# A graph network with attention on one core: own event lists for the first four and the last two iterations, the last batch's heads by transposes, its closing norm on VectorE

## The chip, the core and the metric

The kernel runs on one core of a Trainium2 chip. The metric is device microseconds of one execution. Engines are named as in the profile: PE (TensorE matmuls), PEld (its weight loads), DVE (VectorE), ACT (ScalarE), POOL (GpSimd) and SP, whose queue issues all the DMAs here.

## What is computed

Sixteen batches of 512 nodes with 128 features go through two layers, each with a residual and a layer norm.

```
def euler_step(h, _):                       # eight of them, dt = 1/8
    ax = jnp.einsum('nm,bmd->bnd', adj_mx, h)
    f = alph * 0.5 * (ax - h) + h @ w_eff - h + x0
    return (h + dt * f, None)
...
mask = jnp.where(adj == 0, -jnp.inf, 0.0)
scores = jnp.einsum('bhid,bhjd->bhij', q, k) / np.sqrt(HEAD_DIM) + mask
attn = jax.nn.softmax(scores, axis=-1)      # 4 heads of 32, 512 x 512
out = jnp.einsum('bhij,bhjd->bhid', attn, v)
...
x = _layernorm(x + _L0_gnn_ref(x, adj, ...), axis=-1)
x = _layernorm(x + _L1_gnn_ref(x, L1_gnn_W, adj), axis=-1)
```

The eight Euler steps are linear, so both kernels fold them, ahead of the batches, into powers of the node matrix (tile PTh with its low part PTl) and coefficient matrices (Rh, Rl). That part is called the prologue here.

## The kernel before

**Events.** The work on a batch is cut into events, and each engine walks through its own list of them. An event is (kind, n, i, lag): kind and number, block i of the four blocks of 128 nodes, and the batch as "this iteration minus lag". A label such as S 3 1 of batch 15 stands for head 3, block 1. Engines meet at semaphores only, so a list fixes the order on an engine and the semaphores fix the time. The kinds are:

- Z, XT, C, YT, J: layer 0 (PE, with ACT and DVE taking the results out of PSUM as a high and a low part); UT transposes its result into psM.
- LN1A, LN1B: the first norm (DVE: statistics; POOL: the power -1/2 at L496; DVE: x1 at L1043); KEEP saves x1 on POOL for the residual.
- X1T, Q, K, V: transposed x1 and the three projections; QL, KL their low parts on DVE (L1024). STK: six DMAs for a head that stack the parts of q and k into Qs and Ks (L414).
- S: scores of a block on PE (L772), maximum with mask on DVE (L1055, two banks psS), exponential with row sum on ACT (L586). In this path only the row sum is kept, and the exponential itself is written over Sm.
- MT: the maxima are transposed on PE (L872), split by ACT and DVE into Mh and Ml, and put under Qs by two DMAs (L442).
- TR: the scores once more, transposed and with the maxima already in them (PE L858), mask added by DVE (L1105), exponential by ACT (L631), into ET. So every head is multiplied twice, which spares its 512 x 512 transposes.
- PV: ET times V into psO (L881; it waits at PV 0 for block 0 of the last head), OT: psO to oT on ACT (L637), CB: transpose back (L888) and division (L1119) on DVE.
- ADD: residual on POOL (L506); LN2A: second norm, statistics on DVE (L1030), power and the four y on POOL (L496, L514); OUT: the DMA of y.

**Iterations.** `run_iterations` writes out iterations 0 to 3 from the same list as all others, skipping batches below 0, then a hardware loop over iterations 4 to 13 (two in a body), then 14 and 15 written out, and after them the DRAIN lists. Iteration k does layer 0 of batch k, the scores of batch k-1 and k-2 and the end of k-3, so three batches overlap. In the DRAIN lists TR has four banks (psE and psL, function `late`); elsewhere two.

**Prologue.** ACT converts the node matrix P_sb to Ph (L546), PE transposes it (L720), ACT and DVE split the transposes (L554, L954), POOL makes the low part Pl (L482), and `power` (L688) multiplies. In between, `q_powers` makes powers of a 128 x 128 matrix.

**Masks.** At the end of iteration 0, PE transposes the adjacency matrix (L904), and DVE builds mask (L1128) and maskT (L1131).

## Time and profile before

| | |
|---|---|
| median of 3 runs | 674.31 us (673.86 to 675.66) |
| the profiled execution's own time | 675.34 us |
| its span, first to last instruction | 673.5 us |
| PE busy | 628.7 us (93%) |
| DVE busy | 519.5 us (77%) |
| ACT busy | 459.7 us (68%) |
| POOL busy | 149.4 us (22%) |
| mean granted TensorE clock | 0.972 |

The span is the stretch that the trace covers; 1.8 us of the execution's time lie outside it. A busy share is a mean over stages that differ, so the stages are read apart.

### The profile page before, as it was taken

The page shows a single profiled execution, that of the slowest core. Times are in us where ns is not written, and L with a number is a line of the kernel's source. Part 1 is how long each engine was busy: PE and PEld are TensorE (multiplying, and loading weights), DVE is VectorE, ACT ScalarE, POOL GpSimd, SP SyncE. Part 2 cuts the span into 40 slices and gives each one's busy share as a digit, 9 for nine tenths or more (in the row PEclk, how much of TensorE's full clock was granted, in tenths as well). Part 3 has the DMA queues.
Part 4 walks back from the last instruction along what each step waited for, and adds up shares of the span by engine and source line. Part 5 has one row for each costly group of instructions (what it writes and reads, how often), then busy time and mean ns, then how long its engine had stood idle before and what let it go on. Part 6 is the DMA issues. An engine that isn't in the chain of part 4 may idle for free.

```text
span 673.5 us, 11235 instructions
## 1 busy us (share of the span) xinstructions
PE 628.7 (93%) x3037; PEld 435.6 (65%) x3037; DVE 519.5 (77%) x1406; ACT 459.7 (68%) x1040; POOL 149.4 (22%) x175
## 2 busy tenths in 40 slices
PE   5999888999999999999999999999999999998873
PEld 3777666767666676767676767676767766674330
DVE  4452536879798888888897979797988888889892
ACT  4222035878878686969696868788796868696981
POOL 8010010102112131313040403121121313121205
PEclk9899989999999999999999999999999999999677
DMA  4000012221212221213122221212122223131301
GB/s 113 1 0 17 0 48 63 49 57 44 71 45 65 58 69 51 75 39 86 39 73 52 63 63 47 75 39 71 43 70 55 63 52 76 25 87 36 100 2 31
DMA packets 38205, 35.57 MB, mean 53 GB/s; under 512 B 8096, under 2 KB 25376, under 8 KB 38176
## 3 DMA queue, kind: packets, MB, share of 16 engines
q1 hardware_dynamic: 38176, 35.23, 20.6%
q8 instruction: 13, 0.21, 0.1%
q14 instruction: 16, 0.13, 0.1%
HBM read 5.57 MB, written 4.19 MB: 15 GB/s over the span
## 4 chain that ended last, share of the span: by engine, by line
PE 73%; DVE 14%; issue 4%; DMA 3%; SPq 2%; ACT 1%; POOL 1%; DVEq 0%; POOLq 0%
PE psO L881 8%; PE psS L772 7%; PE psL L758 7%; PE psL L759 7%; PE psE L858 7%; PE psL L760 7%; PE psL L748 4%; PE psL L750 4%; PE psL L749 4%; PE psM L832 4%; DVE ET L1105 4%; DVE x L1043 3%; DMA Ks<-kl 2%; DVE stats L1030 2%; PE psL L823 2%
## 5 line engine op out<-in xcount | busy, mean ns | idle before, releaser
L586 ACT ACTIVATE Sm<-Sm,negmax 128x512 f32<-128x512 f32 x256 | 182.5, 714 | 45.1 <-DVE negmax L1055 44.7
L1055 DVE CUSTOM_DVE_ANT_0 Sm<-psS,mask 128x512 f32<-128x512 f32 x256 | 169.8, 687 | 31.5 <-PE psS L772 25.0
L1105 DVE TENSOR_TENSOR ET<-psE,maskT 128x512 f32<-128x512 f32 x240 | 157.8, 683 | 14.2 <-PE psE L858 13.9
L631 ACT ACTIVATE ET<-ET 128x512 f32<-128x512 f32 x256 | 154.7, 620 | 9.3 <-DVE ET L1105 8.0
L496 POOL TENSOR_TENSOR rstd<-var,minus_half 128x4 f32<-128x4 f32 x32 | 32.7, 1023 | 354.7 <-DVE var L1038 354.7
L858 PE MATMUL psE<-Qs,Ks 98*128 98x512 f32 x240 | 104.8, 459 | 2.6 <-DMA Qs<-Ml 1.0
L772 PE MATMUL psS<-Ks,Qs 96*128 96x512 f32 x256 | 97.8, 423 | 4.6 <-DMA Ks<-kl 4.3
L881 PE MATMUL psO<-ET,V 128*32 128x512 f32 x512 | 65.0, 624 | 0.6 <-ACT ET L631 0.6
L772 PEld LDWEIGHTS psS<-Ks,Qs 96*128 96x128 f32 x256 | 48.4, 192 | 24.1 <-DMA Ks<-kl 8.5
L858 PEld LDWEIGHTS psE<-Qs,Ks 98*128 98x128 f32 x240 | 45.8, 192 | 25.9 <-DVE ET L1105 14.9
L758 PE MATMUL psL<-PTh,Xh 128*128 128x512 f32 x128 | 57.7, 451 | 1.0 <-DVE z L1024 1.0
L748 PE MATMUL psL<-z,Rh 128*128 128x512 f32 x144 | 57.5, 399 | 0.0
L750 PE MATMUL psL<-z,Rl 128*128 128x512 f32 x144 | 56.9, 395 | 0.0
L749 PE MATMUL psL<-z,Rh 128*128 128x512 f32 x144 | 56.9, 395 | 0.0
L758 PE MATMUL psL<-PTh,Yh 128*128 128x512 f32 x128 | 51.6, 404 | 0.1
L514 POOL TENSOR_SCALAR y<-att,mv,rstd 128x128 f32<-128x128 f32 x64 | 50.1, 795 | 4.4 <-POOL rstd L496 4.4
L578 ACT ACTIVATE z<-psL 128x512 fp32r<-128x512 f32 x48 | 28.4, 594 | 33.1 <-PE psL L760 33.1
L759 PE MATMUL psL<-PTl,Xh 128*128 128x512 f32 x128 | 50.8, 397 | 0.0
L760 PE MATMUL psL<-PTh,Xl 128*128 128x512 f32 x128 | 50.7, 396 | 0.0
L759 PE MATMUL psL<-PTl,Yh 128*128 128x512 f32 x128 | 50.5, 395 | 0.0
L760 PE MATMUL psL<-PTh,Yl 128*128 128x512 f32 x128 | 50.5, 395 | 0.0
L586 ACT ACTIVATION_READ_ACCUMULATOR Sm<-Sm,negmax 128x1 f32 x256 | 48.2, 188 | 0.0
(176 smaller groups left out, 972.4 us busy)
## 6 DMA issues: line engine op xcount, KB each, us to landing
Qs<-qh SPq DMA_DIRECT2D x128, 64.0 KB, 2.0
Ks<-kh SPq DMA_DIRECT2D x128, 64.0 KB, 2.0
xin<-in_x_dram SPq DMA_DIRECT2D x16, 256.0 KB, 2.9
Qs<-ql SPq DMA_DIRECT2D x64, 64.0 KB, 2.0
Ks<-kl SPq DMA_DIRECT2D x64, 64.0 KB, 2.0
...
Qs<-Mh SPq DMA_DIRECT2D x32, 4.0 KB
```

What stands on the lines that cost most here:

```text
L586: nc.scalar.activation(row if h < TH else E[:, h % 2, i, :], row, ACT.Exp, scale=-1.0, bias=negmax[:, h * NT + i:h * NT + i + 1], accum_ou ...
L631: nc.scalar.activation(ET[:, n, i, :], ET[:, n, i, :], ACT.Exp, scale=SCALE).then_inc(st_exp, 1)
L748: mm(bank, Rh[:, k, :], zh[:, i, :], start=i == 0, stop=False)
L749: mm(bank, Rh[:, k, :], zl[:, i, :], start=False, stop=False)
L758: mm(bank[:, :], high[:, k, :], PTh[:, i, k, :], start=fresh and k == 0, stop=False)
L759: mm(bank[:, :], high[:, k, :], PTl[:, i, k, :], start=False, stop=False)
L760: last = mm(bank[:, :], low[:, k, :], PTh[:, i, k, :], start=False, stop=k == NT - 1)
L772: mm(psS[i % 2][:, :], Qs[0:KS, h, i * P:(i + 1) * P], Ks[0:KS, h, :], start=True, stop=True).then_inc(s_mm, 1)
L858: last = mm(e_bank(b, n, i)[:, :], Ks[0:KT, n, i * P:(i + 1) * P], Qs[0:KT, n, :], start=True, stop=True)
L881: last = mm(psO[rows, :], V[:, parity, n, rows], ET[:, h, n, :], start=n == 0, stop=n == NT - 1)
L1055: V_.tensor_tensor_reduce(out=Sm[:, i % 2, :], in0=psS[i % 2][:, :], in1=mask[:, i, :], scale=-SCALE, scalar=3e38, op0=ALU.add, op1=ALU.mi ...
L1105: V_.tensor_tensor(ET[:, n, i, :], e_bank(b, n, i)[:, :], maskT[:, i, :], ALU.add).then_inc(t_ev[i % 2], 1)
```

## The change

1. **Lists.** FILL lists give the order for iterations 0 to 3 on every engine, and longer DRAIN lists give that for iterations 14 and 15 and all after. The loop still covers iterations 4 to 13, with a new EVENTS list that starts at another event.
2. **Prologue.** The four conversions to Ph go from ACT to DVE; PE's third `q_powers` goes behind all the transposes, and its result is taken out by DVE.
3. **Masks.** They become four MASK events in the lists of batch 0, each with one quarter of mask and of maskT.
4. **Last batch.** For batch 15 (`moved`) ACT keeps the exponential of S in E. PE transposes E (four 128 x 128 transposes for a TR), and ACT (i even) or DVE (i odd) copies the result into ET. MT, its DMAs, the mask addition and the second exponential of this batch are gone.
5. **Last norm.** ADD and the four y of batch 15 are done by DVE; the power -1/2 stays on POOL.

```diff
+PE_FILL = [
...
+    ("MASK", 0, 0, 0), ("MASK", 1, 0, 0), ("J", 0, 0, 0), ("MASK", 2, 0, 0), ("C", 0, 0, 0), ("YT", 1, 0, 0),
+    ("J", 1, 0, 0), ("MASK", 3, 0, 0), ("UT", 0, 0, 0), ("Z", 1, 0, 1), ("X1T", 0, 0, 0), ("XT", 0, 0, 1),
+    ("Q", 1, 0, 0), ("Z", 2, 0, 1), ("K", 2, 0, 0), ("C", 2, 0, 1), ("C", 1, 0, 1), ("V", 3, 0, 0),
+    ("S", 0, 0, 0), ("S", 0, 1, 0), ("YT", 0, 0, 1), ("S", 0, 2, 0), ("S", 0, 3, 0), ("J", 0, 0, 1),
...
 PE_EVENTS = [
-    ("S", 2, 2, 2), ("PV", 1, 0, 3), ("PV", 2, 0, 3), ("PV", 3, 0, 3), ("UT", 0, 0, 1), ("S", 2, 3, 2),
-    ("TR", 0, 0, 2), ("TR", 0, 1, 2), ("Z", 1, 0, 0), ("XT", 0, 0, 0), ("TR", 0, 2, 2), ("X1T", 0, 0, 1),
...
+    ("TR", 0, 1, 2), ("Z", 1, 0, 0), ("S", 3, 0, 2), ("X1T", 0, 0, 1), ("S", 3, 1, 2), ("TR", 0, 2, 2),
+    ("TR", 0, 3, 2), ("CB", 0, 0, 3), ("Q", 1, 0, 1), ("XT", 0, 0, 0), ("S", 3, 2, 2), ("Z", 2, 0, 0),
+    ("TR", 1, 0, 2), ("K", 2, 0, 1), ("TR", 1, 1, 2), ("TR", 1, 2, 2), ("S", 3, 3, 2), ("C", 2, 0, 0),
...
+    ("MT", 0, 0, 1), ("TR", 3, 3, 2), ("S", 2, 0, 1), ("S", 2, 1, 1), ("J", 1, 0, 0), ("PV", 1, 0, 2),
+    ("UT", 0, 0, 0), ("S", 2, 2, 1), ("PV", 2, 0, 2), ("PV", 3, 0, 2), ("TR", 0, 0, 1), ("S", 2, 3, 1),
...
+MOVED = ((-1, 0), (-1, 1),)
+
+
+def moved(b, h):
+
+    return isinstance(b, int) and (b - B, h // 2) in MOVED
...
     else:
         for kind, n, i, lag in table:
-            b = g * IPG + j - lag
-            if not isinstance(g, int) or b >= 0:
-                yield kind, n, i, b, (j - lag) % IPG
+            yield kind, n, i, g * IPG + j - lag, (j - lag) % IPG
...
-            for t in range(NT):
-                if t == 2:
-                    q_powers(2)
-                act.wait_ge(p_sb, t + 1)
-                nc.scalar.activation(Ph[:, t, :], P_sb[:, t, :], ACT.Copy).then_inc(p_hi, 1)
...
-                nc.scalar.activation(row if h < TH else E[:, h % 2, i, :], row, ACT.Exp, scale=-1.0,
+                nc.scalar.activation(E[:, slot % 2, i, :] if moved(a, h) else row, row, ACT.Exp, scale=-1.0,
...
-                if t < 2:
-                    q_powers(t + 1)
+                if t in (0, NT - 1):
+                    q_powers(1 if t == 0 else 2)
...
+                    elif kind == "MASK":
+                        for t in range(NT):
+                            last = nc.tensor.transpose(P_BANKS[n][:, t * P:(t + 1) * P],
+                                                       adj_sb[:, t, n * P:(n + 1) * P], ident[:, :])
+                        last.then_inc(a_mm, 1)
...
-            for m in range(NT):
-                power_low(0, m)
+            for t in range(NT):
+                dve.wait_ge(p_sb, t + 1)
+                V_.tensor_copy(Ph[:, t, :], P_sb[:, t, :]).then_inc(p_hi, 1)
+            power_low(0, 0)
+            power_low(0, 1)
+            dve.wait_ge(q_mm, 3)
+            V_.tensor_copy(Qp[:, 5:RS, :], psM[:, :].rearrange("p (k d) -> p k d", d=D)).then_inc(q_ev, 1)
+            power_low(0, 2)
+            power_low(0, 3)
...
+                        if isinstance(b, int) and b == B - 1:
+                            dve.wait_ge(x1_kept, b + 1)
+                            dve.wait_ge(c_ev, b + 1 + C_FREE)
+                            V_.tensor_tensor(att[:, :, :], att[:, :, :], x1res[:, parity, :, :],
+                                             ALU.add).then_inc(z_done, 1)
...
+                    elif kind == "LN2B":
+                        dve.wait_ge(y_out, 16 * b + Y_FREE)
+                        normalise(1, b, lambda t: att[:, t, :], lambda t: y[:, t, :]).then_inc(y_done, 1)
```

What the lists make of the program is shown at three places. The first is PE near its start, before the change (rows ahead of the first `power`; psS and psE take the transposes of P_sb, psM the powers of the small matrix):

```order
L661 MATMUL psM<-ET 128x256
L720 MATMUL psS<-ident,E 128x128 x2
L720 MATMUL psE<-ident,E 128x128 x2
L661 MATMUL psM<-ET 128x512
L720 MATMUL psS<-ident,E 128x128 x2
L720 MATMUL psE<-ident,E 128x128 x2
L720 MATMUL psS<-ident,E 128x128 x2
L720 MATMUL psE<-ident,E 128x128 x2
L688 MATMUL psS<-PTh,Qs 128x512 x4
```

The same place of PE in the changed program:

```order
L814 MATMUL psM<-ET 128x256
L873 MATMUL psS<-ident,E 128x128 x2
L873 MATMUL psE<-ident,E 128x128 x2
L873 MATMUL psS<-ident,E 128x128 x2
L873 MATMUL psE<-ident,E 128x128 x2
L873 MATMUL psS<-ident,E 128x128 x2
L873 MATMUL psE<-ident,E 128x128 x2
L814 MATMUL psM<-ET 128x512
L841 MATMUL psS<-PTh,Qs 128x512 x4
```

The 512-column product moved from the middle of the transposes to behind them.

The second place is DVE at the end of batch 0's layer 0, before the change; YT is the result of J 1, and stats<-psM is the start of LN1A:

```order
L1081 TENSOR_TENSOR YT<-psL,biasT 128x512
L1128 TENSOR_SCALAR mask<-E 128x2048
L1131 TENSOR_SCALAR maskT<-psS 128x512 x2
L1131 TENSOR_SCALAR maskT<-psE 128x512 x2
L1030 BN_STATS stats<-psM 128x6 x4
```

The same place of DVE in the changed program, from the low part of YT 1 on:

```order
L1188 TENSOR_TENSOR Yl<-psL,Yh 128x512
L1301 TENSOR_SCALAR mask<-E 128x512
L1304 TENSOR_SCALAR maskT<-psE 128x512
L1161 COPY att<-psM 6x512
L1232 COPY biasT<-psM 128x512
L1245 TENSOR_TENSOR YT<-psL,biasT 128x512
L1301 TENSOR_SCALAR mask<-E 128x512
L1304 TENSOR_SCALAR maskT<-psE 128x512
L1194 BN_STATS stats<-psM 128x6 x4
```

Between YT and the statistics, one mask and one maskT of 512 columns are left of the whole mask and four maskT; two of the other pairs stand further ahead.

The third place is the end of PE's program, before the change: the last TR of batch 15, its PV (16 instructions in one row) and CB:

```order
L858 MATMUL psE<-Qs,Ks 128x512 x2
L858 MATMUL psL<-Qs,Ks 128x512 x2
L881 MATMUL psO<-ET,V 32x512 x16
L888 MATMUL psO<-ident,oT 128x128 x4
L197 UNCONDITIONAL_BRANCH
```

The same place in the changed program, from the last S of batch 15 on:

```order
L925 MATMUL psS<-Ks,Qs 128x512
L1015 MATMUL psL<-ident,E 128x128 x4
L1046 MATMUL psO<-ident,oT 128x128 x4
L1015 MATMUL psL<-ident,E 128x128 x4
L1015 MATMUL psE<-ident,E 128x128 x8
L1015 MATMUL psL<-ident,E 128x128 x4
L1039 MATMUL psO<-ET,V 32x512 x4
L1015 MATMUL psL<-ident,E 128x128 x4
L1039 MATMUL psO<-ET,V 32x512 x12
L1046 MATMUL psO<-ident,oT 128x128 x4
```

Behind the last S only six TR are left (before the change thirteen of the sixteen stand behind it), and the first PV stands ahead of the last TR.

## Rows read from the trace of the kernel before

**Rows 1.** Busy time of each engine by stage, granted clock (PEclk), DMA

```profile
core 0: us, PE busy (x) PEld busy (x) DVE busy (x) ACT busy (x) POOL busy (x), PEclk, DMA share, GB/s
...
80.00:100.00 20.00, 15.04 (x62) 10.49 (x60) 8.21 (x24) 5.94 (x12) 2.88 (x3) 0.91 0.15 36
...
360.00:400.00 40.00, 39.59 (x211) 26.71 (x211) 32.63 (x91) 30.66 (x71) 8.29 (x9) 1.00 0.24 61
...
620.00:640.00 20.00, 15.98 (x51) 6.27 (x50) 18.18 (x51) 18.55 (x46) 4.70 (x6) 0.74 0.38 93
640.00:660.00 20.00, 16.52 (x67) 6.54 (x70) 16.54 (x42) 15.04 (x33) 2.90 (x3) 0.74 0.01 1
660.00:674.00 14.00, 1.79 (x16) 0.55 (x8) 2.11 (x10) 0.60 (x1) 7.93 (x10) 0.73 0.12 37
```

**Rows 2.** Timeline of the prologue: start, duration, instruction, idle before it

```profile
8.76 0.48 DVE L960 TENSOR_SCALAR E<-E,rate 128x512 f32<-128x512 f32 x1
...
9.70 1.67 PE L661 MATMUL psM<-ET 128*128 128x512 f32 x2
...
11.10 5.01 POOL L482 TENSOR_TENSOR z<-E,Qs 128x512 fp32r<-128x512 f32 x4
...
11.90 1.14 ACT L546 ACTIVATE Qs<-E 128x512 fp32r<-128x512 f32 x2
...
15.08 2.05 PE L688 MATMUL psS<-PTh,Qs 128*128 128x512 f32 x4 [2.84 <-ACT PTh L554]
...
20.34 1.25 PE L670 MATMUL psL<-ET 128*128 128x384 f32 x2
```

**Rows 3.** Timeline around the end of batch 0's layer 0

```profile
75.97 0.69 DVE L1081 TENSOR_TENSOR YT<-psL,biasT 128x512 f32<-128x512 f32 x1 [0.77 <-PE psL L760]
...
77.45 0.60 PE L823 MATMUL psM<-ident,YT 128*128 128x128 f32 x4
...
78.91 1.28 DVE L1131 TENSOR_SCALAR maskT<-psE 128x512 f32<-128x512 f32 x2
...
80.22 0.89 DVE L1030 BATCH_NORM_STATS2 stats<-psM 128x6 f32<-128x128 f32 x4
...
84.57 0.63 PE L828 MATMUL psM<-ident,x 128*128 128x128 f32 x4 [3.30 <-DVE x L1043]
...
97.44 0.73 PE L772 MATMUL psS<-Ks,Qs 96*128 96x512 f32 x2 [0.97 <-DMA Ks<-kl]
```

**Rows 4.** Timelines of PE, DVE, SP in one iteration of the loop

```profile
403.89 0.63 PE L828 MATMUL psM<-ident,x 128*128 128x128 f32 x4 [0.38 <-DVE x L1043]
...
409.62 1.02 PE L832 MATMUL psM<-x1T,W_sb 128*128 128x512 f32 x2
...
411.30 0.69 DVE L1024 TENSOR_TENSOR kl<-psM,kh 128x512 fp32r<-128x512 f32 x1
...
413.21 0.59 SPq L414 DMA_DIRECT2D Ks<-kl  x1
...
415.93 0.63 PE L772 MATMUL psS<-Ks,Qs 96*128 96x512 f32 x2
...
431.71 2.78 PE L881 MATMUL psO<-ET,V 128*32 128x512 f32 x24
```

**Rows 5.** Timelines of the tail: scores, last TR, PV, last norm

```profile
646.43 0.69 DVE L1055 CUSTOM_DVE_ANT_0 Sm<-psS,mask 128x512 f32<-128x512 f32 x1
...
649.29 1.27 DVE L1105 TENSOR_TENSOR ET<-psE,maskT 128x512 f32<-128x512 f32 x2
...
655.55 5.59 PE L881 MATMUL psO<-ET,V 128*32 128x512 f32 x32 [0.55 <-ACT ET L631]
...
661.20 0.60 ACT L637 ACTIVATE oT<-psO 128x512 f32<-128x512 f32 x1 [3.37 <-PE psO L881]
...
663.46 1.26 POOL L506 TENSOR_TENSOR att<-att,x1res 128x512 f32<-128x512 f32 x1 [0.94 <-DVE att L1119]
...
667.71 3.12 POOL L514 TENSOR_SCALAR y<-att,mv,rstd 128x128 f32<-128x128 f32 x4 [0.24 <-POOL rstd L496]
```

More of the change, by code:

```diff
@@ L158, with moved_before, schedule @@
 MPB = 4
-def schedule(table, drain, g, j):
-    if isinstance(g, int) and g == NG:
-        for kind, n, i, b in drain:
+MOVED = ((-1, 0), (-1, 1),)
+def moved(b, h):
+    return isinstance(b, int) and (b - B, h // 2) in MOVED
+def moved_before(b, h):
+    return sum(moved(b_, h_) for b_ in range(B - 2, B) for h_ in range(H) if (b_, h_) < (b, h)) \
+        if isinstance(b, int) else 0
+def schedule(fill, table, drain, g, j):
+    if isinstance(g, int) and g in (0, NG):
+        for kind, n, i, b in (drain if g else fill):
             yield kind, n, i, b, b % IPG
@@ L185, in run_iterations @@
             iteration(g, j)
-    for j in range(IPG):
-        iteration(NG - 1, j)
     iteration(NG, 0)
@@ L807, in iteration @@
                             pe.wait_ge(pt_lo, PW * NT)
[L808 removed]
+                        first = isinstance(b, int) and b == 0
                         apply_power(psL[n], Yh, Yl, PW - 1, False,
@@ L877, in iteration @@
                             pe.wait_ge(m_ev, MPB * (b + 1))
-                        pe.wait_ge(st_exp, st_unit(b, TH - 1, n) + 1)
+                        by_matmul = [h for h in range(H) if not moved(b, h)]
+                        if by_matmul:
+                            pe.wait_ge(st_exp, st_unit(b, by_matmul[-1], n) + 1)
+                        if moved(b, H - 1):
+                            pe.wait_ge(*eviction(b, H - 1, n))
                         for h in range(H):
@@ L899, in iteration @@
                             bias_rows(2)
-                if isinstance(g, int) and g == 0 and j == 0:
-                    for m in range(NT):
-                        for t in range(NT):
-                            last = nc.tensor.transpose(P_BANKS[m][:, t * P:(t + 1) * P],
-                                                       adj_sb[:, t, m * P:(m + 1) * P], ident[:, :])
-                        last.then_inc(a_mm, 1)
             run_iterations(pe, iteration)
```

128 lines of the change are left out of this document (77 added, 51 removed), and 226 rows, old and new, of tables (ACT_DRAIN, ACT_EVENTS, ACT_FILL, DVE_DRAIN).

## The prediction

> **What bounds the kernel now.** I read the busy time by stage first [rows 1]. From about 160 us to 610 us the program is in its steady part: PE is busy 39.59 of 40 us, DVE 32.63, ACT 30.66. PE bounds it there, at a granted clock of 1.00, that is 2.4 GHz. The reader should see next where this fails. From 80 to 100 us PE is busy 15.04 of 20 us and the clock is 0.91. From 620 to 640 us it is busy 15.98 us at a clock of 0.74 while DVE is busy 18.18 and ACT 18.55, and from 660 us on nearly nothing is on PE. So the kernel has one long stretch with little to win, and three places where another engine sets the pace: the prologue, the first batch, and the tail from 611 us on. The timelines of these places [rows 2, 3, 5] show who is waited for, and one iteration of the loop [rows 4] shows the margins of the steady part.
>
> The sums are made against the profiled execution, 675.34 us, which is 1.03 us above the median of 674.31 us; I take that off at the end. A difference under 0.3% (2.0 us) can't be told from no change here.
>
> **The prologue.** PE waits 2.84 us before its first `power` at 15.08 us, for ACT, and all twelve products of it take until 20.34 us, 5.26 us or 0.44 us each [rows 2]. In the steady part the same shape costs 0.23 us, so these run at 1.2 GHz: the clock fell while PE stood still. ACT is late because it makes Ph as well (two of the four in 1.14 us, until 13.04 us) and because the 512-column product (1.67 us from 9.70 us on) stands between the transposes it waits for. After the change ACT has only the four high parts to make. The transposes lose that product from their midst and end about 1.5 us sooner, at 10.6 us; four high parts at 0.55 us give 12.85 us. DVE gets four conversions; the trace shows no such one on DVE. Below, a 128x512 operation of DVE on SBUF took 0.48 us [rows 2], above, one that reads PSUM takes 0.60 to 0.69 us [rows 5]. I take 0.48, the row with the same operands: 1.9 us from 9.6 us on, then two low parts, the product's result and two low parts at 0.6 to 0.65 us each, which ends at 14.7 us (15.4 at the upper price; now 16.04). The next cover is POOL: Pl takes 5.01 us from 11.10 us, starts behind POOL's own memsets and so does not move; it ends at 16.11 us. PE's last four products can't start before that, so the first `power` ends at 17.1 us at the full clock, 18.4 us at the half clock, against 20.34 us. Everything behind it on PE is dense until 80 us. Gain 1.9 to 3.2 us; I take **2.6**.
>
> **The first batch.** UT ends on PE at 78.05 us, but DVE starts the statistics at 80.22 us, because the masks stand ahead of them [rows 3]. X1T then starts at 84.57 us after 3.30 us of idle PE. After the change only one mask pair (about 0.3 + 0.64 us) is left between YT and the statistics. Three mask transposes of 0.44 us now stand ahead of J 1 and no longer hide YT's way through DVE, so UT moves by +0.5 us relative to the work before it and the statistics start at about 78.85 us. That is 1.4 us sooner, and everything up to Q follows. XT of batch 1 moves behind X1T, where it fills the time in which ACT copies x1T; the idle time ahead of X1T stays above 1.5 us. V now stands ahead of S 0 0 and covers the 0.97 us wait for the stacked Ks [rows 3] with 0.9 us of work. The clock fell behind this idle time, to a mean of 0.91 from 80 to 100 us [rows 1]; with less idle time it may stay up, which is worth at most 9% of 20 us, 1.8 us. Bounds 1.3 and 4.1 us, I take **2.9**: both waits, and a third of the clock.
>
> **The steady part.** In each iteration PE loses 0.38 us at X1T, which waits for x1 [rows 4]. Now PV 2, PV 3 and S 3 0 stand between UT and X1T and XT behind it: cover goes from 4.2 to 6.0 us. The way over DVE becomes longer by one maximum, 0.7 us, and stays hidden. But TR 1 2 now follows TR 1 0 after only K and TR 1 1, some 0.8 us, and needs the bank that DVE empties at least 1.0 us after TR 1 0; that gives back 0.2 to 0.4 us. And X1T's copy on ACT now has one more exponential ahead of it, which can hold Q for 0.1 to 0.3 us. J 1 to UT has only PV 1 (0.93 us, a third of 2.78 [rows 4]) to cover about 0.95 us of YT on DVE. Best case 0.5 us less in each of 13 iterations, 6.5 us; worst case of these small items 0.3 us more, 4 us. I take 0.15 us less, **2.0** in all, as the gain at X1T is a row and the others are margins.
>
> **The tail.** From 620 to 656.5 us DVE works almost without a gap [rows 1]. The last maximum ends at 647.1 us [rows 5]; behind it come fourteen mask additions at 0.60 us (649.29: two in 1.20), then PV from 655.55 us, which took 5.59 us in place of the 3.7 us of the steady part [rows 4, 5], then oT at 661.20 us. So from the last maximum to oT it is 14.1 us.
> - Removed for batch 15: 16 additions (9.6 us of DVE), 16 exponentials (8.3 us of ACT at 0.52), two MT with their DMAs. Added: 8 copies on DVE, which the trace doesn't show for this pair of tiles (another operation PSUM to SBUF takes 0.60 to 0.69 us; I take 0.60), 8 on ACT at 0.5 to 0.6 us, and 64 transposes on PE for 16 products, 0.44 against 0.23 us per block, 3.4 us at the full clock.
> - Up to the last maximum, DVE has all TR of batch 14 as now, four copies in place of two additions and no MT: about +0.6 us. PE has four to five more transposed blocks there. At the half clock a head costs PE 4 x 0.45 + 4 x 0.9 = 5.4 us against 4 us on DVE, so PE can hold the others in part: I take the last maximum **1.3 us later** (0.6 to 3).
> - Behind the last maximum T: exponential T + 0.95, three TR of 0.44, PV 0 when ACT has copied TR 3 0 (T + 2.6), the last TR, three more PV: oT at T + 7.1 at the full clock, T + 9.8 at the half clock. Statistics of batch 14 stand ahead of DVE's last copy, which is at T + 5.1, and hold PV 3 in neither case. I take T + 7.9, so this is 14.1 - 7.9 = **6.2 us** less.
> - Last norm: ADD goes from 1.26 us and its two handovers on POOL to 0.7 us on DVE, 0.7 us less; four y go from 3.12 us to four DVE operations of 0.4 us (x1 at L1043 is the same operation on the same sizes, 1.36 us), 1.7 us less: **2.4 us**. The DMA of y 14 must have landed before; POOL gives it out some 9 us behind T and it needs 2.9 us, while y 15 starts near T + 13.
> - SP: OUT of batch 13 stands ahead of the stacks of head 2 and needs no wait, as LN2A 13 is earlier on DVE.
>
> Tail: 1.3 - 6.2 - 2.4 = **-7.3 us**, bounds -4 and -10.
>
> **Sum.** -2.6 - 2.9 - 2.0 - 7.3 = -14.8 us; 675.34 - 14.8 - 1.03 = 659.5 us.
>
> **The page on the clock.** Behind the last S, PE does transposes almost alone. What a low clock costs is in the rows: PV took 5.59 us in the tail against 3.7 us. "TensorE: Matmul & The Clock Gate" of the Trainium skill, section on PE-mode transpose, says that transposes don't count as PE activity for the clock in the way that matmuls do. By that rule the clock would stay at 1.2 GHz from batch 15's first TR on, and the time would be the second rival's. No row of before has transposes for long enough to say.
>
> **The rivals.**
> 1. **Steady part at its best.** The wait at X1T goes and nothing takes its place: -6.5 in place of -2.0, 655 us. For it: 0.38 us with its name in each iteration. Against it: the TR 1 2 margin. Chance 0.17.
> 2. **The tail stays at 1.2 GHz.** T another 1.7 us later, oT at T + 9.8 in place of 7.9, CB slower: +4 to +5 us, 664 us. For it: 0.74 in the tail now, with gaps on PE. Against it: PE has fewer gaps after the change. Chance 0.22.
> 3. **Small waits in the new order.** Bubbles at TR 1 2, Q and UT outweigh X1T by 0.3 us an iteration: +4 in place of -2, 665.5 us. Chance 0.10.
> 4. **The stack of Ks becomes late (slower).** KL starts 1.68 us behind K, its last DMA is given out at 413.21 us and takes 0.59 + 2.0 us: it lands at 415.80 us, and S 0 0 starts at 415.93 us [rows 4]. The margin is 0.1 us, and ACT's and DVE's new lists put more exponentials and maxima near K and KL. Each 0.7 us of one such operation ahead of KL would stand on PE's path in each of 13 iterations, 9 us. Two of them are 18 us, more than the 12.8 us of the other terms: 675.34 - 12.8 + 18 - 1.03 = 679.5 us. It decides from 1.0 us an iteration on. Against it: the list has four products, two blocks of C and three TR between K and S 0 0, as now. Chance 0.05 for slower, 0.03 for about equal.
>
> **Chances.** The forecast itself (656 to 663 us) has 0.43. Rivals 1, 2 and 3 are all faster by far more than 0.3%: faster 0.92, same 0.03, slower 0.05. The range goes from the first rival (655 us) with tail and first batch near their better bounds (2.7 and 1.2 us more), 650.5 us, most of the way to the second and third rival together (670 us), 668.5 us.
>
> **What would show it.** Prologue: the first `power` ends at 17 to 18.5 us and not at 20.3. First batch: statistics of LN1A start about 4 us earlier in absolute time than 80.2, and no wait of 0.97 us at the first S. Steady: X1T has no wait for DVE, and an iteration is up to 0.4 us shorter; a wait at S 0 0 for Ks would be the fourth rival. Tail: from the last maximum to oT 7 to 10 us, from oT to the end 9.9 us (now 12.3). The prediction is wrong if an iteration becomes longer by over 0.5 us, or if T moves by more than 5 us against the last J.

## The result

The changed kernel takes 658.79 us (median of 5, 658.19 to 659.55) against 675.07 us of the kernel before on the same chip (median of 5, 673.86 to 675.79). The ratio is 0.976, 95% interval 0.9748 to 0.9774, so it is 15 to 17 us faster. The forecast was 659.5 us, 650.5 to 668.5. The profiled execution took 659.55 us with a span of 657.8, against 675.34 and 673.5 before: 15.8 us less, and the parts below are measured against that. Later, in the runs beside after_again, one execution of the changed kernel took 1544.67 us and one of the kernel before 882.92 us; they count in no comparison.

The busy times by stage of the kernel after, which answer to [rows 1] (columns as there):

```profile
core 0: us, PE busy (x) PEld busy (x) DVE busy (x) ACT busy (x) POOL busy (x), PEclk, DMA share, GB/s
80.00:100.00 20.00, 17.09 (x76) 12.36 (x75) 8.08 (x19) 8.60 (x18) 2.15 (x3) 1.00 0.26 67
...
620.00:640.00 20.00, 18.39 (x100) 10.68 (x100) 16.45 (x43) 18.22 (x44) 2.06 (x3) 0.81 0.27 69
640.00:658.00 18.00, 7.25 (x59) 3.49 (x57) 9.10 (x33) 3.50 (x8) 6.45 (x7) 0.82 0.10 29
```

PE is busy 2 us more of 20 in the first batch and 2.4 more in the tail, each at a higher clock. The stretch from 660 us on, with 1.8 us of PE in 14, is gone.

**Prologue.** Timelines of PE, POOL and DVE after the change (start, duration, instruction, idle time before it), for [rows 2]:

```profile
12.77 1.17 PE L841 MATMUL psS<-PTh,Qs 128*128 128x512 f32 x4 [1.01 <-ACT PTh L704]
...
17.18 2.07 PE L841 MATMUL psS<-PTh,z 128*128 128x512 f32 x4 [1.48 <-POOL z L635]
19.05 1.39 PE L823 MATMUL psL<-ET 128*128 128x384 f32 x2
...
10.45 0.38 POOL L624 MEMSET minus_half<- 128x4 f32 x1
...
12.01 5.12 POOL L635 TENSOR_TENSOR z<-E,Qs 128x512 fp32r<-128x512 f32 x4
...
9.60 1.85 DVE L1125 CAST Qs<-E 128x512 fp32r<-128x512 f32 x4
...
14.37 4.11 DVE L1097 SCALAR_TENSOR_TENSOR ET<-ET 128x128 f32<-128x128 f32 x9
```

PE's wait for ACT ahead of the first power shrank from 2.84 to 1.01 us, and DVE's four conversions take 0.46 us each. But Pl (here under its buffer's name z) starts at 12.01, not 11.10 us, and PE's last four products wait for it until 17.18. The first power ends 1.3 us sooner (20.34 to 19.05).

**First batch.** Timelines of PE and DVE after the change, for [rows 3]:

```profile
76.89 0.66 PE L976 MATMUL psM<-ident,YT 128*128 128x128 f32 x4 [0.42 <-DVE YT L1245]
...
77.80 0.89 DVE L1194 BATCH_NORM_STATS2 stats<-psM 128x6 f32<-128x128 f32 x4
...
82.14 0.63 PE L981 MATMUL psM<-ident,x 128*128 128x128 f32 x4 [1.80 <-DVE x L1207]
...
93.67 0.73 PE L925 MATMUL psS<-Ks,Qs 96*128 96x512 f32 x2 [0.34 <-DMA Ks<-kl]
...
108.23 0.66 PE L976 MATMUL psM<-ident,YT 128*128 128x128 f32 x4 [0.55 <-DVE YT L1245]
```

X1T waits 1.80 us in place of 3.30, the first S 0.34 in place of 0.97. UT of batch 1 stands at 108.23; before the change:

```profile
112.04 0.66 PE L823 MATMUL psM<-ident,YT 128*128 128x128 f32 x4 [0.56 <-DVE YT L1081]
...
220.39 0.66 PE L823 MATMUL psM<-ident,YT 128*128 128x128 f32 x4
...
541.39 0.66 PE L823 MATMUL psM<-ident,YT 128*128 128x128 f32 x4
...
611.12 0.66 PE L823 MATMUL psM<-ident,YT 128*128 128x128 f32 x4 [0.31 <-DVE YT L1081]
```

That is 3.8 us up to here, of which XT of batch 0 (52.45 before, 51.30 after) already has 1.15; the first batch is the other 2.66.

**Steady part.** PE's timeline after: UT at the start and the end of nine iterations of the loop, UT of batch 15, and X1T of batch 10.

```profile
213.57 0.65 PE L976 MATMUL psM<-ident,YT 128*128 128x128 f32 x4
...
531.87 0.33 PE L976 MATMUL psM<-ident,YT 128*128 128x128 f32 x1
...
603.13 0.66 PE L976 MATMUL psM<-ident,YT 128*128 128x128 f32 x4 [0.31 <-DVE YT L1245]
...
432.28 0.60 PE L981 MATMUL psM<-ident,x 128*128 128x128 f32 x4
```

Nine iterations took (541.39 - 220.39) / 9 = 35.67 us each and take 35.37. X1T has no wait, where it had 0.38 us [rows 4]. From UT of batch 1 to that of 15 it was 499.1 us and is 494.9: 4.2 us less.

**Tail.** Timelines of DVE, ACT and POOL after the change, for [rows 5]:

```profile
639.67 0.69 DVE L1219 CUSTOM_DVE_ANT_0 Sm<-psS,mask 128x512 f32<-128x512 f32 x1 [0.17 <-PE psS L925]
...
649.58 0.69 DVE L1285 TENSOR_TENSOR att<-psO,rec 128x512 f32<-128x512 f32 x1 [3.81 <-POOL y L669]
650.38 0.69 DVE L1292 TENSOR_TENSOR att<-att,x1res 128x512 f32<-128x512 f32 x1
...
653.93 1.11 DVE L1207 TENSOR_SCALAR y<-att,mv,rstd 128x128 f32<-128x128 f32 x4 [1.22 <-POOL rstd L649]
...
647.17 0.60 ACT L790 ACTIVATE oT<-psO 128x512 f32<-128x512 f32 x1 [3.73 <-PE psO L1039]
...
646.37 3.12 POOL L669 TENSOR_SCALAR y<-att,mv,rstd 128x128 f32<-128x128 f32 x4 [0.24 <-POOL rstd L649]
```

The last maximum ends at 640.36 us, oT starts at 647.17, and the span ends at 657.8: from maximum to oT 6.8 us (before 14.1), from oT to the end 10.6 (before 12.3). One wait is new: the last division waits 3.81 us, and the profile names POOL's four y of batch 14, which read att until 649.49.

### The profile page after: what moved, and what is told of

It is laid out like the page before. It is cut to its first block, busy times and chain, and to the rows that moved or that the text cites. A ratio compares the mean times of both kernels' runs of the same rounds, so it can differ in the third digit from the quotient of the medians.

```text
span 657.8 us, 11313 instructions
## 1 busy us (share of the span) xinstructions
PE 624.2 (95%) x3083; PEld 434.4 (66%) x3083; DVE 524.1 (80%) x1409; ACT 452.1 (69%) x1025; POOL 146.3 (22%) x170
## 4 chain that ended last, share of the span: by engine, by line
PE 84%; DVE 6%; POOL 3%; issue 2%; DMA 2%; ACT 1%; SPq 1%; POOLq 0%; DVEq 0%
PE psL L911 9%; PE psL L912 9%; PE psL L913 9%; PE psE L1011 9%; PE psO L1039 8%; PE psS L925 8%; PE psM L985 4%; PE psL L901 4%; PE psL L902 4%; PE psL L903 4%; PE psL L976 2%; PE psM L990 2%; DMA Ks<-kl 2%; PE psE L841 2%; DVE ET L1269 2%
## 5 line engine op out<-in xcount | busy, mean ns | idle before, releaser
L1219 DVE CUSTOM_DVE_ANT_0 Sm<-psS,mask 128x512 f32<-128x512 f32 x256 | 172.4, 686 | 31.1 <-PE psS L925 22.3
L737 ACT ACTIVATE Sm<-Sm,negmax 128x512 f32<-128x512 f32 x240 | 171.4, 716 | 24.9 <-DVE negmax L1219 24.4
L1269 DVE TENSOR_TENSOR ET<-psE,maskT 128x512 f32<-128x512 f32 x232 | 154.4, 683 | 13.4 <-PE psE L1011 12.7
L782 ACT ACTIVATE ET<-ET 128x512 f32<-128x512 f32 x240 | 144.2, 620 | 19.5 <-DVE ET L1269 19.2
L925 PE MATMUL psS<-Ks,Qs 96*128 96x512 f32 x256 | 102.4, 432 | 5.8 <-DMA Ks<-kl 3.4
L1011 PE MATMUL psE<-Qs,Ks 98*128 98x512 f32 x232 | 94.6, 456 | 1.3
L1011 PEld LDWEIGHTS psE<-Qs,Ks 98*128 98x128 f32 x232 | 43.0, 191 | 33.4 <-issue 13.9
L911 PE MATMUL psL<-PTh,Xh 128*128 128x512 f32 x128 | 51.6, 403 | 1.0 <-DVE z L1188 1.0
L669 POOL TENSOR_SCALAR y<-att,mv,rstd 128x128 f32<-128x128 f32 x60 | 47.0, 794 | 4.1 <-POOL rstd L649 4.1
L659 POOL TENSOR_TENSOR att<-att,x1res 128x512 f32<-128x512 f32 x15 | 19.5, 1297 | 116.9 <-DVE att L1285 116.9
```

What stands on the lines that cost most here:

```text
L737: nc.scalar.activation(E[:, slot % 2, i, :] if moved(a, h) else row, row, ACT.Exp, scale=-1.0, bias=negmax[:, h * NT + i:h * NT + i + 1], ...
L782: nc.scalar.activation(ET[:, n, i, :], ET[:, n, i, :], ACT.Exp, scale=SCALE).then_inc(st_exp, 1)
L911: mm(bank[:, :], high[:, k, :], PTh[:, i, k, :], start=fresh and k == 0, stop=False)
L925: mm(psS[i % 2][:, :], Qs[0:KS, h, i * P:(i + 1) * P], Ks[0:KS, h, :], start=True, stop=True).then_inc(s_mm, 1)
L1011: last = mm(e_bank(b, n, i)[:, :], Ks[0:KT, n, i * P:(i + 1) * P], Qs[0:KT, n, :], start=True, stop=True)
L1219: V_.tensor_tensor_reduce(out=Sm[:, i % 2, :], in0=psS[i % 2][:, :], in1=mask[:, i, :], scale=-SCALE, scalar=3e38, op0=ALU.add, op1=ALU.mi ...
```

## The experiments

All are edits of the changed kernel. The ratios are each against the kernel before, run beside it on the same chip (674.84 us for experiments 1 to 4, 674.6 for 5 to 8, 676.22 for 9 to 12); 0.001 of the ratio is 0.67 us. A ratio has an interval of 0.0013 to 0.002 on either side, so what differs by less than some 1.5 us is told from the positions in the traces, not from the times.

| kernel | us, median (range) | ratio, 95% | first power ends | UT 15 | UT 15 to last max. | to oT | oT to end |
|---|---|---|---|---|---|---|---|
| before | 675.07 (673.86-675.79) | 1 | 20.34 | 611.12 | 36.0 | 14.1 | 12.3 |
| changed | 658.79 (658.19-659.55) | 0.976, 0.9748-0.9774 | 19.05 | 603.13 | 37.2 | 6.8 | 10.6 |
| old_tail | 667.94 (666.69-674.48) | 0.9902, 0.9884-0.992 | 18.64 | 608.66 | 37.0 | 14.7 | 12.3 |
| undo_ln2 | 661.54 (660.57-662.35) | 0.9807, 0.9789-0.9825 | 18.10 | 601.93 | 37.0 | 6.8 | 13.4 |
| own_att | 659.0 (657.25-659.14) | 0.9762, 0.9743-0.978 | 17.92 | 602.5 | 38.5 | 6.8 | 9.5 |
| late_ut | 675.38 (674.94-680.95) | 1.0019, 1.0-1.0037 | 18.13 | 617.9 | 38.4 | 6.9 | 10.6 |
| undo_prologue | 660.78 (659.94-662.64) | 0.9798, 0.9776-0.982 | 20.55 | 604.36 | 37.2 | 6.8 | 10.6 |
| ph_on_act | 659.03 (657.79-659.21) | 0.9761, 0.9742-0.978 | 17.26 | 601.5 | 38.5 | 6.8 | 10.6 |
| pool_first | 659.92 (659.78-660.81) | 0.9786, 0.9767-0.9805 | 17.99 | 603.45 | 37.1 | 6.8 | 10.6 |
| masks_behind | 662.78 (662.14-665.13) | 0.9829, 0.9806-0.9853 | 18.15 | 605.18 | 38.4 | 6.8 | 10.6 |
| after_again | 660.44 (659.47-1544.67) | 0.977, 0.9755-0.9786 | 18.08 | 603.18 | 38.0 | 6.8 | 10.6 |
| best | 656.35 (655.48-658.56) | 0.9725, 0.9705-0.9746 | 17.26 | 600.81 | 37.2 | 6.8 | 9.5 |
| best_cover | 654.73 (653.48-655.15) | 0.9691, 0.9676-0.9706 | 17.27 | 598.37 | 37.0 | 6.8 | 9.5 |

The last five columns are positions and distances in us in each kernel's trace. The first power is taken to end where PE's next products, into psL, start; UT 15 is the transpose of layer 0's result of batch 15, and the end is that of the span.

**1. old_tail: the tail of before behind the new start and loop.** PE's list stands here for all five; ADD and y of batch 15 go back to POOL with the edit of undo_ln2, below.

```diff
 PE_DRAIN = [
...
-    ("S", 3, 3, 15), ("TR", 2, 2, 15), ("CB", 0, 0, 14), ("TR", 2, 3, 15), ("TR", 3, 0, 15), ("TR", 3, 1, 15),
-    ("TR", 3, 2, 15), ("PV", 0, 0, 15), ("TR", 3, 3, 15), ("PV", 1, 0, 15), ("PV", 2, 0, 15), ("PV", 3, 0, 15),
...
+    ("TR", 0, 2, 15), ("S", 3, 3, 15), ("TR", 0, 3, 15), ("MT", 1, 0, 15), ("TR", 1, 0, 15), ("TR", 1, 1, 15),
+    ("TR", 1, 2, 15), ("TR", 1, 3, 15), ("TR", 2, 0, 15), ("TR", 2, 1, 15), ("TR", 2, 2, 15), ("TR", 2, 3, 15),
...
-MOVED = ((-1, 0), (-1, 1),)
+MOVED = ()
```

> The changed kernel with the DRAIN lists of before, in their order: the last batch's heads by a second product with maxima in it, mask addition and second exponential, and its last ADD and four y on POOL. Prologue, first four iterations and loop stay changed. Theory (tail worth 7.7 us by the traces): the time goes up from 658.8 to about 666.5 us, the last maximum ends some 36 us behind the transpose of u of batch 15 and oT comes 14 us behind that maximum. Rival (the earlier arrival at the tail and the clock there make the gain, not the lists and the transposes): 659 to 661 us. Rival 2 (the old tail is worse at its new place, since the clock falls at another point): above 669 us.

Measured: ratio 0.9902, 9.5 us above the changed kernel by the ratios. From UT of batch 15 to the end of the span it is 64.0 us against 54.6, 9.4 us more: 7.9 between the last maximum and oT, 1.7 behind oT, -0.2 ahead. PE's timeline there has what the change removed:

```profile
649.30 1.22 PE L1010 MATMUL psE<-Qs,Ks 98*128 98x512 f32 x2 [0.45 <-DMA Qs<-Ml]
...
654.19 6.13 PE L1038 MATMUL psO<-ET,V 128*32 128x512 f32 x32 [0.56 <-ACT ET L781]
```

The first rival (little gain in the tail) falls; the theory holds, with a larger size, and the second rival has a part in it (the granted clock from 620 to 660 us is 0.66 here, 0.74 before the change). The edit takes back the lists, the transposes and the last norm together: undo_ln2 tells the norm from the rest, no run tells the lists from the transposes. The profiled execution was this kernel's longest, 674.48 us, and one reason lies apart from the edit: from 15 to 32 us its granted clock was 0.60, where the changed kernel's was low for some 3.5 us only, and UT of batch 0 came 5 us later (81.83 against 76.89).

**2. undo_ln2: ADD and the four y of batch 15 on POOL again.**

```diff
-                        if isinstance(b, int) and b == B - 1:
-                            dve.wait_ge(x1_kept, b + 1)
-                            dve.wait_ge(c_ev, b + 1 + C_FREE)
-                            V_.tensor_tensor(att[:, :, :], att[:, :, :], x1res[:, parity, :, :],
-                                             ALU.add).then_inc(z_done, 1)
...
-                        if isinstance(b, int) and b == B - 1:
-                            continue
                         pool.wait_ge(root[1], b + 1)
```

> The changed kernel, but ADD and the four y of batch 15 are POOL's again. Theory (the prediction's): +2.4 us, ADD 1.26 with its handovers in place of 0.69 us and four y at 3.12 in place of 1.11 us, so 661.2 us. Rival (the new wait of 3.81 us that the last division has for POOL's y of batch 14 stays in both, and hides nothing): the same +2.4 to +2.7. Rival 2 (DVE's y gains nothing, as the DMA of y sets the end): under +0.7 us.

Measured: 3.1 us slower by the ratios, 2.8 us more between oT and the end (13.4 against 10.6). POOL's timeline:

```profile
649.07 1.26 POOL L658 TENSOR_TENSOR att<-att,x1res 128x512 f32<-128x512 f32 x1 [0.94 <-DVE att L1282]
...
653.32 3.13 POOL L666 TENSOR_SCALAR y<-att,mv,rstd 128x128 f32<-128x128 f32 x4 [0.24 <-POOL rstd L648]
```

With DVE it is 0.69 and 1.11 us, and only the handover for the power -1/2 is left. The edit is worth the 2.4 us that was predicted for it and a little more, and the new wait stands in both kernels.

**3. own_att: nothing of batch 15 waits for POOL's y of batch 14.**

```diff
-                        if after_first(b):
+                        last_one = isinstance(b, int) and b == B - 1
+                        att_b = x1 if last_one else att
+                        if last_one:
+                            dve.wait_ge(x1_kept, b + 1)
+                        elif after_first(b):
                             dve.wait_ge(y_done, b)
```

> The last division of the heads, ADD and the second norm of batch 15 work in tile x1 and in the first norm's small tiles, which are free by then, so that nothing of batch 15 waits for POOL's four y of batch 14. Theory (the miss of 0.7 us between oT and the end is this wait): the division starts 1.0 us sooner, 1.4 us behind oT as before the change, and the time is 657.8 us. Rival (POOL's queue: the power -1/2 of batch 15 stands behind those y too, and they slow DVE while both run): 658.5 to 658.9 us.

Measured: ratio 0.9762, no change of time. The trace of it does show the theory's mechanism in DVE's timeline, the division 1.35 us behind oT (2.41 in the changed kernel) and waiting for PE only, and 1.1 us less from oT to the end:

```profile
649.12 0.69 DVE L1295 TENSOR_TENSOR x<-psO,rec 128x512 f32<-128x512 f32 x1 [2.72 <-PE psO L1047]
```

What took it back is ahead of it: the last maximum stands 38.5 us behind UT of batch 15 instead of 37.2. The windows of this kernel's tail, and below of the changed kernel's, show why:

```profile
630.00:637.00 7.00, 6.14 (x46) 4.23 (x38) 5.14 (x13) 5.94 (x16) 0.00 (x0) 1.00 0.12 29
637.00:641.00 4.00, 3.55 (x16) 3.29 (x17) 2.43 (x9) 3.14 (x9) 0.00 (x0) 0.61 0.00 0
```

```profile
630.00:637.00 7.00, 6.40 (x50) 4.36 (x42) 4.93 (x14) 5.95 (x15) 0.00 (x0) 1.00 0.12 30
637.00:641.00 4.00, 3.05 (x23) 2.55 (x22) 3.43 (x11) 4.00 (x11) 0.00 (x0) 1.00 0.00 0
```

PE's order is the same there; the clock fell to 1.2 GHz behind PE's waits at the last S in one execution and not in the other. The row below is from that stretch of own_att; the same eight transposes took 1.04 us in the changed kernel, at 2.4 GHz:

```profile
637.79 1.84 PE L1016 MATMUL psE<-ident,E 128*128 128x128 f32 x8
```

Two other traces, with 38.5 and 38.4 us (ph_on_act, late_ut), have such a second low stretch (the expectation of after_again, below, counts four; masks_behind has none). All traces with the new tail have a first one, from some 14 to 18 us behind UT 15 on, for 7 to 10 us; masks_behind (38.4) and after_again (38.0) have that one late and long. So one profile decides nothing about 1.3 us here.

**4. late_ut: only UT moved back behind PV 3, in the loop.**

```diff
-    ("UT", 0, 0, 0), ("S", 2, 2, 1), ("PV", 2, 0, 2), ("PV", 3, 0, 2), ("TR", 0, 0, 1), ("S", 2, 3, 1),
+    ("S", 2, 2, 1), ("PV", 2, 0, 2), ("PV", 3, 0, 2), ("UT", 0, 0, 0), ("TR", 0, 0, 1), ("S", 2, 3, 1),
```

> Only PE's list of the loop is changed: the transpose of u goes from behind PV 1 to behind PV 3, as before the change, so 4.0 us of products instead of 6.0 stand between it and X1T, in ten iterations. The way from UT over statistics, power and x to X1T took 5.9 us in the changed kernel's trace. Theory (the gain in the loop comes from the cover ahead of X1T): X1T waits some 1.3 us or more in each of ten iterations that begin in the loop, +10 to +14 us, 669 to 673 us, with DVE's x named as what PE waits for. Weaker form: DVE's and POOL's lists make the way shorter again when UT comes later, +0.4 us an iteration, 663 us. Rival (the gain comes from other places of the new order): no more than +1 us, under 660 us.

Measured: 675.38 us, 17 us slower than the changed kernel by the ratios, so this one move costs more than the whole change brings. PE's timeline of one iteration, then all of X1T by what ended its idle times (us, times):

```profile
399.54 0.66 PE L976 MATMUL psM<-ident,YT 128*128 128x128 f32 x4
...
405.37 0.63 PE L981 MATMUL psM<-ident,x 128*128 128x128 f32 x4 [1.43 <-DVE x L1207]
```

```profile
its engine sat idle before it (us, times) until:
  issue: 19.7, 12
  DVE x L1207: 14.8, 11
```

X1T waits 1.36 to 1.43 us in each of nine iterations, with x named, and an iteration is 37.0 us against 35.37. From UT to X1T it is 5.83 us here; in [rows 4]'s kernel it was 5.20 (398.69 to 403.89). So the new DVE list made the way 0.6 us longer, as the prediction had it (one more maximum), and what covers it is the work that PE's new list puts ahead of X1T. Without that cover the new lists are worse than the old.

**5. undo_prologue and 6. ph_on_act.** The first puts the conversions on ACT and the third product of `q_powers` back between the transposes; the second moves only the conversions:

```diff
+            for t in range(NT):
+                act.wait_ge(p_sb, t + 1)
+                nc.scalar.activation(Ph[:, t, :], P_sb[:, t, :], ACT.Copy).then_inc(p_hi, 1)
...
-            for t in range(NT):
-                dve.wait_ge(p_sb, t + 1)
-                V_.tensor_copy(Ph[:, t, :], P_sb[:, t, :]).then_inc(p_hi, 1)
```

> The changed kernel with the prologue of before: the four conversions to Ph on ACT, the third product of q_powers between the transposes and taken out by ACT. Theory (traces: the first power ends 1.3 us sooner after the change, XT of batch 0 1.15 us): 659.9 to 660.1 us. Rival (a later start brings the first batch's clock to another place): 658.5 or above 661 us.

> Only the four conversions to Ph go back to ACT; the product of q_powers stays behind the transposes. Theory (DVE's conversions on SBUF slow POOL's memsets, so that Pl starts at 12.0 and not at 11.1 us): POOL's Pl starts at 11.1 us again and ends near 16.1 us, but ACT is late with its high parts (12.9 + 2.0 us), so the first power ends within 0.5 us of the changed kernel's 19.05 us. Rival (POOL is late for another reason): Pl starts at 12.0 us here too, and the first power ends at 19.5 to 20 us.

Measured: undo_prologue is 2.5 us slower by the ratios (1.2 us by the positions at UT 15), and its first power ends at 20.55 us. ph_on_act has POOL's memsets and Pl where they were before the change, and all of `power` at the full clock, done at 17.26 us:

```profile
10.16 0.10 POOL L624 MEMSET minus_half<- 128x4 f32 x1
...
11.14 5.03 POOL L635 TENSOR_TENSOR z<-E,Qs 128x512 fp32r<-128x512 f32 x4
...
16.28 1.14 PE L844 MATMUL psS<-PTh,z 128*128 128x512 f32 x4
```

So it is DVE's conversions that hold POOL (theory), and they were not needed: with them on ACT the first power starts later (13.63 us, against 12.77 to 13.21 in the traces with the changed kernel's prologue) but has no wait for Pl. What makes the prologue faster is the product moved behind the transposes, with its result taken out by DVE; the two kernels differ in both, and no run tells them apart. The time of ph_on_act is still the changed kernel's (ratio 0.9761); its trace is 1.6 us ahead at UT 15 and has lost 1.2 of them at the last maximum, by the second low stretch. The memset of minus_half takes 0.10 us without DVE's conversions beside it and 0.38 us with them. The "SBUF — State Buffer" page of the Trainium skill, section "Who interferes with whom", says that a cast on VectorE can run in a mode that takes a pair of SBUF ports shared with GpSimd, and that the one that issues first then holds the pair for its whole instruction and blocks the other. By that rule, and the trace agrees in direction, Pl would not have stayed at 11.10 us; no run here shows in which mode the conversions ran.

**7. pool_first: POOL makes Pl before its memsets.**

```diff
+            pool.wait_ge(p_sb, NT)
+            for t in range(NT):
+                pool.wait_ge(p_hi, t + 1)
+                nc.gpsimd.tensor_tensor(Pl[:, t, :], P_sb[:, t, :], f(Ph[:, t, :]),
+                                        ALU.subtract).then_inc(p_lo, 1)
             nc.gpsimd.memset(bcols[:, :], 0.0).then_inc(c_pool, 1)
```

> The changed kernel, but POOL makes Pl before its other small work (memsets and weight casts), which ran for some 1.8 us ahead of it. Theory (POOL's Pl is what the last four products of the first power wait for): Pl ends at 15.3 us instead of 17.1, the first power 1.8 us sooner at the half clock or 2.6 us sooner if the clock stays up, so 656.2 to 657.0 us. Rival (DVE's PTl, or POOL's postponed work, is late next): under 0.7 us gained.

Measured: 1.7 us slower by the ratios (1.1 us against after_again), where the theory had some 2 us less, so the rival. Its timelines of POOL and DVE:

```profile
9.96 5.40 POOL L623 TENSOR_TENSOR z<-E,Qs 128x512 fp32r<-128x512 f32 x4 [2.31 <-DVE Qs L1125]
...
9.38 3.58 DVE L1125 CAST Qs<-E 128x512 fp32r<-128x512 f32 x4
```

POOL gains 1.8 us, but DVE's four conversions take 3.58 us beside it instead of 1.85; DVE's low parts are late next, and the first power ends at 17.99 us, where others with a full clock have 17.9 to 18.2. The 1.7 us are hardly more than the intervals of the two ratios, and nothing at the first power explains them. A half-clock stretch at 81 to 85 us is in its trace (X1T of batch 0 to UT 1: 27.2 us against 26.1), but own_att has one too (27.3 us), without being slower. What else makes the difference, if it is one, stays open.

**8. masks_behind: the four mask pieces together ahead of the statistics.**

```diff
 PE_FILL = [
...
-    ("MASK", 0, 0, 0), ("MASK", 1, 0, 0), ("J", 0, 0, 0), ("MASK", 2, 0, 0), ("C", 0, 0, 0), ("YT", 1, 0, 0),
-    ("J", 1, 0, 0), ("MASK", 3, 0, 0), ("UT", 0, 0, 0), ("Z", 1, 0, 1), ("X1T", 0, 0, 0), ("XT", 0, 0, 1),
+    ("J", 0, 0, 0), ("C", 0, 0, 0), ("YT", 1, 0, 0), ("J", 1, 0, 0), ("MASK", 0, 0, 0), ("MASK", 1, 0, 0),
+    ("MASK", 2, 0, 0), ("MASK", 3, 0, 0), ("UT", 0, 0, 0), ("Z", 1, 0, 1), ("X1T", 0, 0, 0), ("XT", 0, 0, 1),
```

> The changed kernel, but in the lists of the first batch all four mask pieces stand together ahead of LN1A, as before the change. Theory (the masks ahead of the statistics cost the first batch its wait): the statistics start about 1.4 us later against J 1, X1T waits for x some 3.3 us in place of 1.80, and the time is 660.2 us, or up to 661.5 us if the clock falls behind the longer wait. Rival (the gain of the first batch comes from the order behind X1T, with XT and V as fillers): under +0.6 us.

Measured: 4.6 us slower by the ratios, three times what I expected (3.2 us by the spans of the two traces, of which 1.2 lie in the tail, where its low stretch is late). DVE's and PE's timelines:

```profile
73.33 0.69 DVE L1245 TENSOR_TENSOR YT<-psL,biasT 128x512 f32<-128x512 f32 x1 [0.78 <-PE psL L913]
...
77.78 0.89 DVE L1194 BATCH_NORM_STATS2 stats<-psM 128x6 f32<-128x128 f32 x4
...
82.14 0.63 PE L981 MATMUL psM<-ident,x 128*128 128x128 f32 x4 [3.94 <-DVE x L1207]
```

The statistics stand 4.45 us behind YT, against 1.66 in the changed kernel (76.14 to 77.80), and X1T waits 3.94 us, not the 3.3 of before, as XT of batch 1, which stood ahead of X1T before the change, stands behind it here. Behind that wait the granted clock is 0.83 from 80 to 90 us (1.00 in the changed kernel). UT 0 to UT 1 is 35.05 us against 31.34: 3.7 us, of which 2.1 are ahead of X1T. UT 0 itself comes 0.6 us sooner against the first power than in after_again, as the mask transposes stand behind J 1 there and fill the time in which YT is made, so UT 1 is 2.7 us later: 91.7 us behind the first power against 89.0.

**9. transposes: which clock is granted under transposes alone.** 400 extra transposes, whose results nobody uses, stand first.

```diff
+            for n in range(400):
+                nc.tensor.transpose(psE[n % 2][:, 0:P], ident[:, :], ident[:, :])
             nc.tensor.transpose(psM[:, 0:D], w_sb[:, :], ident[:, :]).then_inc(c_pe, 1)
```

> 400 transposes of the 128 x 128 identity into the two banks psE stand ahead of PE's program, so its time is longer by them; it is run to see which clock is granted while PE does transposes alone and without a gap. Theory (the rows of the last batch: transposes ran at 2.4 GHz there, but with products between them): the granted clock is 1.00 over most of the stretch, a transpose takes 0.11 us or less, and the time grows by some 25 us. Rival (the page's rule, transposes don't count as activity): the clock falls to 0.50 in the stretch and stays there, a transpose takes 0.21 us, and the time grows by over 45 us.

Measured: 703.59 us. PE's timeline of them, and the windows with the granted clock behind the five engines:

```profile
4.61 44.74 PE L807 MATMUL psE<-ident 128*128 128x128 f32 x397
```

```profile
35.00:50.00 15.00, 14.45 (x133) 14.21 (x131) 0.51 (x3) 0.00 (x0) 0.00 (x0) 1.00 0.00 1
50.00:58.00 8.00, 4.67 (x24) 2.89 (x24) 7.33 (x16) 2.73 (x6) 3.36 (x3) 1.00 0.00 0
58.00:66.00 8.00, 7.38 (x21) 5.29 (x21) 5.32 (x17) 1.52 (x4) 2.00 (x2) 0.57 0.00 0
```

The clock is 2.4 GHz through 44.7 us in which PE does nothing but transposes, 0.112 us each, and falls to 1.2 GHz only behind the wait of 2.67 us ahead of the first power. The rival falls. The time grew by 43 us against after_again's, not by the 25 us of the theory, but that was an error of its sum: 400 times 0.112 us is 45 us, and it would be 84 us by the rival's 0.21 us. The prediction's second rival rested in part on the rule that transposes don't keep the clock up; this run and the tail speak against it for transposes of this size.

**10. after_again, 11. best, 12. best_cover.** best has the edits of own_att and ph_on_act together. best_cover adds transposes whose results nobody uses, in PE's two early waits:

```diff
+            def cover(n):
+                for _ in range(n):
+                    nc.tensor.transpose(psO[:, 0:P], ident[:, :], ident[:, :])
...
+            cover(8)
             power(1, 0)
...
                     elif kind == "X1T":
+                        if isinstance(b, int) and b == 0:
+                            cover(13)
                         pe.wait_ge(x1_done, b + 1)
```

> The changed kernel once more, beside the combined versions on the same chip. The eight traces so far differ in where the clock fell: a half-clock stretch of 3 to 4 us between 637 and 641 us was there in four of them and put the last maximum 38.4 us behind the transpose of u of batch 15, where the others have 37.1. Theory: the same kernel shows either, by chance, and its times lie between 658 and 660 us. Rival: the changed kernel itself always has 37.1 to 37.3 us.

> The changed kernel with two edits that were each run alone: the last division, ADD and second norm of batch 15 in tile x1 (nothing waits for POOL's y of batch 14), and the four conversions to Ph on ACT (POOL's Pl starts 0.9 us sooner). Theory by the traces: 1.0 us less from oT to the end and 0.7 us less at the first power, 657.1 us against 658.8. Rival (each alone measured the same as the changed kernel, as the clock falls at other places and takes it back): 658.5 to 659.2 us.

> The version above, and PE does transposes of the identity into psO in its two early waits: eight ahead of the first power, thirteen ahead of X1T of batch 0 (their results are used by nobody). Theory (the clock falls behind these waits in some executions, 14 to 31 us in one and 81 to 85 us in four of the traces, and transposes keep it up): no granted clock under 1.00 before 600 us, less spread, and 0.3 to 0.8 us off the median, 656.5 us. Rival (transposes don't keep the clock up, or they hold the products behind them): the same as the version above or up to 1 us slower.

Measured: the changed kernel itself has 38.0 us from UT 15 to the last maximum this time. Its low stretch in the tail is as long as in the first profile (10 us) but lies 1.8 us later against UT 15, and there is no second one; neither theory nor rival of after_again had this, but the distance differs by 0.8 us in one and the same kernel. Its times are 659.5 to 660.6 us, 0.6 us above those of the result by the ratios. best is 3.0 us below after_again by the ratios (theory 1.7), best_cover 5.3 us below. It is the fastest of all, 654.73 us, and its five times lie within 1.7 us of each other, those of best within 3.1. PE's timeline of best_cover in the first batch:

```profile
77.78 1.58 PE L875 MATMUL psO<-ident 128*128 128x128 f32 x13
79.67 0.66 PE L992 MATMUL psM<-ident,x 128*128 128x128 f32 x4 [0.31 <-DVE x L1220]
```

From 5 to 120 us no granted clock under 1.00 stands in its trace, but that is so in five traces without cover too, best among them. Its trace is 2.4 us ahead of best at UT 15, but not for the clock: best waits 0.72 and 0.96 us for the stack of Ks at its first two places, best_cover for neither, which is 1.7 of the 2.4 us. Why that stack lands sooner there, and whether cover did it, these runs don't tell. That the covers gain through the clock is therefore open.

## Why the prediction came out right

**Prologue: 2.6 predicted, 1.3 in the profile, some 2.2 in most traces.** One step failed. "Pl [...] starts behind POOL's own memsets and so does not move; it ends at 16.11 us" is wrong: it ended at 17.13, as the new conversions on DVE slow the memsets (ph_on_act undoes just that). What stood ahead of Pl was priced well: ACT's high parts ended at 12.67 us (12.85 predicted), DVE's low parts at 14.45 (14.7). So "17.1 us at the full clock, 18.4 us at the half clock" became 17.9 to 18.2 us in the five traces with this prologue and a full clock, and 19.05 in the profiled one, where the clock was low: 0.8 to 1.1 and 0.65 us later than said, where Pl was 1.0 us late. The whole part is worth 2.5 us by the times of undo_prologue.

**First batch: 2.9 predicted, 2.66 in the profile.** UT moved by +0.5 us and the wait at X1T shrank by 1.5, as said; the clock stayed at 1.00 where it had been 0.91 [rows 1]. V did not remove the wait at the first S, which is 0.34 us here and 0 to 0.72 in other traces. The statistics start 2.4 us earlier than before the change, not the 4 us that the prediction named as a sign (3.9 in after_again, where the clock stayed up in the prologue). masks_behind shows that the place of the masks alone is worth 3.7 us from UT 0 to UT 1, in the new order, or 2.7 us when UT 0's own delay is counted: as much as the whole part. What V and XT bring there was not run apart.

**Steady part: 2.0 predicted, 4.2 in the profile.** The mechanism is the predicted one (late_ut), but the term was undersized: 0.15 us an iteration, where 0.30 was measured. The 0.38 us at X1T went whole. Of the small items set against it none shows: in nine iterations PE stands idle 0.7 us in all ahead of TR products (0.8 before), and not at Q or the first S. How well 4.2 us stands for the part is less sure: from UT of batch 1 to that of 15 the same kernel took 496.1 us in after_again, 3.0 us less than before, though its iterations of the loop take 35.40 us each; the rest lies ahead of the loop and behind it. I had halved a gain that a row showed for margins that no row showed.

**Stack of Ks (slower rival).** In the changed kernel no such wait stands between 130 and 550 us, as forecast; 0.32 us stand at 551 us (0.47 before, at 559). In the tail it stands: 1.83 us ahead of S 0 0 of batch 15 (1.61 before), and the first low stretch of the clock begins within this wait, at 617.5 us:

```profile
618.03 1.22 PE L925 MATMUL psS<-Ks,Qs 96*128 96x512 f32 x2 [1.83 <-DMA Ks<-kl]
```


**Tail: 7.3 predicted, 7.8 in the profile.** Last maximum 1.2 us later (1.3 predicted); that it fits so well is luck, as the other traces with this tail have 1.0 to 2.5 us, by where the clock fell. From it to oT 7.3 us less (6.2 predicted): T + 7.1 was given for the full clock, and it was T + 6.8, as the transposes ran at 2.4 GHz. Behind oT 1.7 us less (2.4 predicted): the edit is worth 2.8 us (undo_ln2), and the wait of the division for POOL's y of batch 14, which the text took for hidden ("must have landed before" spoke of the DMA only), gives 1.1 us back (own_att). By old_tail the tail is worth 9.4 us, 1.6 more than the two traces differ by, since the old tail at its new place is itself 1.6 us longer than before the change (64.0 against 62.4 us), with a granted clock of 0.66 in place of 0.74 from 620 to 660 us.

The sum of the profile is 1.15 + 2.66 + 4.2 + 7.8 = 15.8 us against 14.8: the prologue was over by 1.4, the loop under by 2.2, the rest within 0.5. So the time is right in part because two misses cancel. One slip of the recorded sums: the bounds named for the lower end of the range give 651.1 us, not 650.5, and nothing hangs on it.
